# Spreading x by 128-partition transfers, and taking a block's rows and lookups later in the slot, in a recommender tower on one core

## The reference

```
e = stack([tbl_f[ids[:, f]] for f in range(32)], axis=1)      # (1024, 32, 16)
z_i[f, g] = x0[f] * h[g];  y = relu(W_i @ z_i + b_i)          # 128 outputs
layer 0: h = x (32 rows);  layer 1: h = upper half of y0 (64);  layer 2: h = upper half of y1 (64)
kept: lower halves of y0 and y1, all of y2; summed over the 16 columns e -> 256 values
h = concat([kept, dense_ctx (16)]); h = relu(h @ W_top1 + b); h = relu(h @ W_top2 + b); y = h @ W_top3
```

## Time and profile before

| | us |
|---|---|
| runs of the kernel before | 1099.53, 1104.21, 1105.62; median 1104.21 |
| the profiled execution | 1104.94, span 1103.1 |
| busy: PE | 1003.6 (91%) |
| busy: DVE | 840.5 (76%) |
| busy: POOL | 822.1 (75%) |
| busy: ACT | 470.1 (43%) |
| mean granted clock of PE, as a share of full speed | 0.969 |
| moved by DMA | 184.54 MB, mean 167 GB/s |

### The profile page before, as it was taken

The page is one execution under the profiler, slowest core; times in us unless marked ns, Lnnn a source line. Parts: engine busy times, 40 slices in busy tenths (PEclk is TensorE's granted clock), DMA queues, the critical chain, the costliest instruction groups (busy, mean ns, idle before and its releaser), DMA issues.

```text
span 1103.1 us, 11677 instructions
## 1 busy us (share of the span) xinstructions
PE 1003.6 (91%) x3089; PEld 572.8 (52%) x3089; DVE 840.5 (76%) x747; ACT 470.1 (43%) x587; POOL 822.1 (75%) x524
## 2 busy tenths in 40 slices
PE   3257889999997999998999989998899999999998
PEld 2223445555554555554555545554455555555565
DVE  5234768887785889888688869888478878888882
ACT  0123444444443444444345444444344444444453
POOL 6645778887877978887898878887788866656650
PEclk9579999999998999999999999999899999999999
DMA  6079989899896888899988899899688998999300
GB/s 119 10 159 208 200 174 205 188 194 193 168 195 139 184 180 186 183 196 190 184 172 185 186 182 184 182 191 196 143 179 179 195 202 188 192 198 196 86 1 0
DMA packets 111813, 184.54 MB, mean 167 GB/s; under 512 B 19571, under 2 KB 24179, under 8 KB 111541
## 3 DMA queue, kind: packets, MB, share of 16 engines
q1 hardware_dynamic: 103604, 182.24, 78.4%
q0 software_dynamic: 8192, 2.11, 2.0%
HBM read 181.15 MB, written 3.15 MB: 167 GB/s over the span
## 4 chain that ended last, share of the span: by engine, by line
POOL 38%; issue 28%; PE 23%; DVE 4%; SPq 2%; DMA 2%; ACT 1%; POOLq 0%; DVEq 0%
POOL low L490 22%; PE y L605 14%; POOL looked_up L480 13%; PE y L613 5%; PE y L628 3%; POOL tail_parts L498 2%; DMA spread<-xcols 1%; DVE unsplit L1046 1%; DVE prod L1046 1%; SPq L406 1%; SPq L424 1%; DVE low L1054 0%; PE xT L577 0%; PE y L709 0%; DMA xcols<-xrows 0%
## 5 line engine op out<-in xcount | busy, mean ns | idle before, releaser
L490 POOL TENSOR_TENSOR low<-unsplit,high 128x1024 fp32r<-128x1024 f32 x221 | 530.8, 2408 | 149.2 <-ACT high L809 145.8
L605 PE MATMUL y<-prod,w1T 128*128 128x512 f32 x1024 | 481.2, 598 | 5.0 <-ACT kept L801 2.7
L1046 DVE TENSOR_TENSOR prod<-spread,h 128x1024 f32<-128x1024 f32 x288 | 346.0, 1211 | 84.2 <-PE y L605 65.6
L809 ACT CAST high<-unsplit 128x1024 fp32r<-128x1024 f32 x224 | 233.9, 1046 | 293.4 <-DVE unsplit L1046 288.8
L1046 DVE TENSOR_TENSOR unsplit<-spread,h 128x1024 f32<-128x1024 f32 x224 | 271.3, 1211 | 100.1 <-ACT h L795 100.1
L480 POOL DMA_INDIRECT looked_up<-in_tbl,ids_now x256 | 249.1, 973 | 75.1 <-issue 66.8
L605 PEld LDWEIGHTS y<-prod,w1T 128*128 128x128 f32 x1024 | 193.3, 192 | 166.0 <-issue 145.3
L613 PE MATMUL y<-high,w2T_high 128*128 128x512 f32 x448 | 226.7, 506 | 6.6 <-ACT high L809 6.6
L628 PE MATMUL y<-low,w2T_high 128*128 128x512 f32 x448 | 207.0, 543 | 27.6 <-POOL low L490 27.3
L613 PE MATMUL y<-high,w2T_low 128*128 128x512 f32 x448 | 178.4, 398 | 0.0
L795 ACT ACTIVATE h<-y,bias 64x512 f32<-64x512 f32 x128 | 83.3, 651 | 165.4 <-PE y L605 161.4
(11 more groups left out here) (112 smaller groups left out, 418.6 us busy)
## 6 DMA issues: line engine op xcount, KB each, us to landing
spread<-xcols SPq DMA_DIRECT2D x256, 512.0 KB
shifted<-xcols SPq DMA_DIRECT2D x124, 256.0 KB
shifted_tail<-xcols SPq DMA_DIRECT2D x124, 64.0 KB
looked_up<-in_tbl,ids_now POOLq DMA_INDIRECT x256
xcols<-xrows SPq DMA_DIRECT2D x32, 96.0 KB
spread<-in_L_rec_W SPq DMA_DIRECT2D x3, 512.0 KB, 3.9
spread<-in_L_rec_W SPq DMA_DIRECT2D x1, 1024.0 KB
wt<-in_W_top SPq DMA_DIRECT2D x2, 512.0 KB, 10.1
```

Source lines behind the costliest of these rows:

```text
L490: pool.tensor_tensor(low[kind][r][:, :, :], unsplit[kind][r][:, :, :], high[kind][r][:, :, :].bitcast(F32), ALU.subtract).then_inc(s_low[k ...
L605: last = pe.matmul(y[:, :], w, z[:, c, :], start=(n == 0 and c == 0), stop=(item in (LAST0, LAST1) and c == ITEM - 1))
L809: act.copy(high[kind][r][:, :, :], unsplit[kind][r][:, :, :]).then_inc(s_high[kind], 1)
L1046: dve.tensor_tensor(z, x[:, ITEM * n:ITEM * (n + 1), :], b[:, :].unsqueeze(1).to_broadcast([P, ITEM, COLS]), ALU.mult).then_inc(s_made[kin ...
```

## The change

It has two parts, made together.

The first spreads x otherwise. In a group of four chunks each partition reads four rows of x that lie one behind the other in DRAM, 8 KB in one piece, by one DMA over all 128 partitions. Partition p of chunk c now has field c + 2 * (p // 8), modulo 32. Eight neighbouring partitions read the same bytes. The pairs of a field and a row of h are the same 2048 in another order, so the columns of W1 and W2 are put in that order before PE turns them: SP loads each with its first fields again behind the last (wrapped, 46 fields), and ACT makes eight copies of 128 x 512 into the prod buffers, from which PE turns. shifted likewise takes pieces of 8 KB, still by four DMAs of 32 partitions, and W0's arrangement and the first tile's factors (L1007) follow it.

The second moves work within the slot. ACT takes a block's rows and repeats the fields behind (2,2) instead of (2,0). In a block's first slot POOL begins the block behind (2,2) and TAIL, and makes two lookups behind each of (2,3), (2,4), (2,5) and (2,7). In the other three it makes two lookups ahead of all items, none behind (2,0) and (2,1), one behind (2,2), two behind (2,3), and one behind each of (2,4), (2,5), (2,7).

```diff
-LOOKUPS_AFTER = (0, 2, 2, 1, 1, 1, 1)
+LOOKUPS_AFTER = ((0, 0, 0, 2, 2, 2, 2), (0, 0, 1, 2, 1, 1, 1))
+LOOKUPS_FIRST = (0, 2)
...
-                for half in range(2):
-                    sp.dma_start(spread[k % 2][HALF * half:HALF * (half + 1), GROUP * g:GROUP * (g + 1), :],
-                                 bass.AP(x.tensor, x.offset + (2 * GROUP * g + half) * COLS,
-                                         [[0, HALF], [2 * COLS, GROUP], [1, COLS]])
-                                 ).then_inc(s_spread[k % 2][g], 16)
+                sp.dma_start(spread[k % 2][:, GROUP * g:GROUP * (g + 1), :],
+                             bass.AP(x.tensor, x.offset + GROUP * g * COLS,
+                                     [[2 * COLS, P // RUN], [0, RUN], [1, GROUP * COLS]])
+                             ).then_inc(s_spread[k % 2][g], 16)
...
                     sp.dma_start(shifted[FIELDS * j:FIELDS * (j + 1), :, :],
-                                 bass.AP(x.tensor, x.offset + j * COLS,
-                                         [[COLS, FIELDS], [GROUP * COLS, GROUP], [1, COLS]])
+                                 bass.AP(x.tensor, x.offset + GROUP * j * COLS,
+                                         [[COLS, FIELDS], [1, GROUP * COLS]])
...
+                if mine:
+                    look_up_some(LOOKUPS_FIRST[quarter > 0])
                 for n, item in enumerate(mine):
                     split_low(s, item)
                     if TAIL in items and item == (2, 2):
                         split_tail(s)
-                    if n == 1 and left and quarter == 0:
+                    if item == (2, 2) and left and quarter == 0:
                         begin(b)
-                    if n >= 1:
-                        for _ in range(LOOKUPS_AFTER[n]):
-                            if left:
-                                look_up(FIELDS // TILES_PER_BLOCK * quarter + left.pop(0))
+                    look_up_some(LOOKUPS_AFTER[quarter > 0][n])
...
+            for r, (raw, s_w, landed) in enumerate(((w1_raw, s_w1, 64), (w1_raw, s_w1, 64), (w2_raw, s_w2, 32), (w2_raw, s_w2, 32))):
+                act.wait_ge(s_w, landed)
+                for half in range(2):
+
+                    first = (2 * GROUP * (r % 2) + CHUNKS * half) * HALF
+                    last = act.copy(w_turned[r].rearrange("p (c h i j) -> p h c i j", h=2, i=HALF // RUN, j=RUN)[:, half],
+                                    bass.AP(raw.tensor, raw.offset + first,
+                                            [list(raw.ap[0]), [HALF, 2 * GROUP], [2 * HALF + RUN, HALF // RUN], [1, RUN]]))
+                last.then_inc(s_ordered, 1)
             act.wait_ge(s_biases, 5 * 16)
...
-                ready_after = (2, 0) if (2, 0) in items else (0, 0)
+                ready_after = (2, 2) if (2, 2) in items else (0, 0)
...
-                        dve.wait_ge(s_spread[t[1] % 2][n // (GROUP // ITEM)], 32 * uses_of_parity(t))
+                        dve.wait_ge(s_spread[t[1] % 2][n // (GROUP // ITEM)], 16 * uses_of_parity(t))
```

More of the change, by code:

```diff
@@ L53 @@
 COPY = 32
+RUN = 8
+WRAP = FIELDS - 2
 BYTES = 4
@@ L341, in dlrm_tower @@
         flat = lambda ap: ap.rearrange("p a b -> p (a b)")
[L342 to L345, removed]
+        w1_raw = flat(spread[0][:, 0:6, :])
+        w2_raw = flat(spread[0][:, 6:12, :])
+        w0_raw = flat(spread[0][:, 12:14, :])
+        w0_wide = flat(spread[1][:, 9:13, :])
         w0_dist = flat(spread[0][:, 14:16, :])
+        w_turned = [flat(prod[r][:, :, :]) for r in range(4)]
         dense_wide = flat(spread[1][:, 0:2, :]).rearrange("p (n c) -> p n c", c=P)
@@ L369, in _ @@
             sp.dma_start(w0_raw, w0[:, :]).then_inc(s_w0, 16)
-            sp.dma_start(w1_raw[0:HALF, :], w1[HALF:P, :]).then_inc(s_w1, 16)
-            sp.dma_start(w1_raw[HALF:P, :], w1[0:HALF, :]).then_inc(s_w1, 16)
-            sp.dma_start(w2_raw, w2[:, :]).then_inc(s_w2, 16)
+            ALL, MORE = FIELDS * HALF, (CHUNKS + WRAP - FIELDS) * HALF
+            for to, of in ((slice(0, ALL), slice(0, ALL)), (slice(ALL, ALL + MORE), slice(0, MORE))):
+                sp.dma_start(w1_raw[0:HALF, to], w1[HALF:P, of]).then_inc(s_w1, 16)
+                sp.dma_start(w1_raw[HALF:P, to], w1[0:HALF, of]).then_inc(s_w1, 16)
+            for to, of in ((slice(0, ALL), slice(0, ALL)), (slice(ALL, ALL + MORE), slice(0, MORE))):
+                sp.dma_start(w2_raw[:, to], w2[:, of]).then_inc(s_w2, 16)
             for to, of in ((bias0[HALF:P, :], b0[HALF:P]), (bias1[0:HALF, :], b1[HALF:P]),
@@ L508, in slot, with look_up_some @@
                 mine = of_kind(items, BY_POOL, plan.is_last(s))
+                def look_up_some(count):
+                    for _ in range(count):
+                        if left:
+                            look_up(FIELDS // TILES_PER_BLOCK * quarter + left.pop(0))
                 if TAIL in items and not mine:
                     split_tail(s)
+                if mine:
+                    look_up_some(LOOKUPS_FIRST[quarter > 0])
                 for n, item in enumerate(mine):
@@ L549, in _ @@
             pe.wait_ge(s_ident, 1)
-            pe.wait_ge(s_sym, 7)
+            pe.wait_ge(s_sym, 10)
             turn(0, GROUP, P, lambda c: w0_dist[:, P * c:P * (c + 1)])
             turn(1, 1, P, lambda c: w0_dist[:, P * GROUP:P * (GROUP + 1)])
-            pe.wait_ge(s_w1, 32)
-            for g in range(GROUPS):
-                turn(2 + g, GROUP, P, lambda c: w1_raw[:, P * (GROUP * g + c):P * (GROUP * g + c + 1)])
-            pe.wait_ge(s_w2, 16)
-            for g in range(GROUPS):
-                turn(2 + GROUPS + g, GROUP, P, lambda c: w2_raw[:, P * (GROUP * g + c):P * (GROUP * g + c + 1)])
+            for g in range(2 * GROUPS):
+                pe.wait_ge(s_ordered, g // 2 + 1)
+                turn(2 + g, GROUP, P, lambda c: w_turned[g // 2][:, P * (GROUP * (g % 2) + c):P * (GROUP * (g % 2) + c + 1)])
             pe.wait_ge(s_stored, PREP_GROUPS)
@@ L940, in _ @@
             H = FIELDS // 2
-            dve.tensor_copy(w0_dist[:, FIELDS:FIELDS * H].rearrange("p (d f) -> p d f", f=FIELDS),
-                            bass.AP(w0_wide.tensor, w0_wide.offset + 1,
-                                    [list(w0_wide.ap[0]), [1, H - 1], [2 * FIELDS + 1, FIELDS]])).then_inc(s_sym, 1)
+            for a in range(GROUP):
+                dve.tensor_copy(w0_dist[:, P * a:P * (a + 1)].rearrange("p (j f) -> p j f", f=FIELDS),
+                                bass.AP(w0_wide.tensor, w0_wide.offset + a,
+                                        [list(w0_wide.ap[0]), [GROUP, GROUP], [2 * FIELDS + 1, FIELDS]])).then_inc(s_sym, 1)
+            dve.wait_ge(s_sym, 3)
             dve.tensor_copy(w0_dist[:, 0:FIELDS], diagonal(w0_raw, FIELDS, 0, FIELDS)).then_inc(s_sym, 1)
@@ L1007, in _ @@
                 dve.tensor_copy(rotated[c].rearrange("p (e a f) -> p e a f", a=GROUP, f=FIELDS),
[L1008 to L1009 removed]
+                                bass.AP(unwrapped.tensor, unwrapped.offset + (c if c < GROUP else FIELDS // 2),
+                                        [list(unwrapped.ap[0]), [XROWS, QUAD], [GROUP if c < GROUP else 0, GROUP], [1, FIELDS]])
                                 ).then_inc(s_rotated, 1)
```

5 lines of the change are left out of this document (2 added, 3 removed).

## The result

The changed kernel takes 1094.53 us (median of 6 runs, 1093.26 to 1095.37), the kernel before 1103.08 beside it (6 runs): a ratio of 0.9921, with a 95% interval of 0.9896 to 0.9946. That is faster by 8.6 us, where I had forecast 29. It lies in the range of 1061 to 1096, but the likeliest case was wrong: less than a third of the gain came, and the time is that of rival (2). The profiled execution has a span of 1092.8, 10.3 less than before.

The account below looks back on a forecast made before the run. POOL was taken to lose time in waits, leaving 44.2 us above PE's floor of 29.31 per slot. Slots -20.5, filling -9, start 0: together -29.5 from 1104.9, predicting 1075 us, range 1061 to 1096.

Parts of the forecast that it names:

- the likeliest case: The forecast itself: 1075 us, its own range 1068 to 1085, chance 0.53.
- rival (2): Transfers stay at 213 GB/s, bound by rereading the same bytes; filling gains 0, stands stay 9.1: 1093 us; 0.14 with late ACT.
- The blocks: Slots of five blocks: 3.1 us per block above the floor instead of up to 5.8, 15.5 in all, between 9 and 22.
- held third slot: Block's third slot: DVE's addition held behind POOL's two low parts, POOL idles 5.1, low (2,2) late by 1.25 us.
- new stall in the second slot: Block's first two slots: low (2,7) 0.7 us late, then lookups ahead make low (2,0) 1.15 late.
- Rival (1): DVE's addition is let in behind one low part, so no third slot is held: 1067.5 us, chance 0.10.
- The transfers: Spread of x over 128 partitions moves at 370 GB/s instead of 213, bounds 213 and 385.
- The filling: While the pipeline fills, faster transfers shorten DVE's waits for shifted: 9 us less, bounds 0 and 14.2.
- The start: Extra weight loads and ACT's eight copies stay covered by the wait for first rows: 0; 14.5 us if ACT starts late.
- The stands: POOL's waits before lookups 114 and 227 shorten: slot 8 costs 3.0 instead of 9.4, slots 22 to 24 5.2 instead of 11.2.

Follow-up runs that it names:

- one_between: Changed kernel with one lookup of every plain slot moved from after GpSimd's fourth subtraction to between its first and second: 1081.97 us, ratio 0.9856 to before.
- o_plain: Kernel before with the change's block's first slot and ACT's copies behind (2,2), but old transfers and old lookups in the three plain slots: 1080.01 us, ratio 0.9786.
- src_rows: Changed kernel with the spread reading 128 different 8 KB rows of W1 in place of x: 1077.0 us (one run).
- src_reread: Changed kernel with the spread reading W1 in place of x, in the change's pattern of 8 partitions per stretch: 1090.1 us (one run).
- both_kept: o_plain with VectorE's addition of the kept part later (after (2,2)) and the change's transfers and reordered weights: 1063.83 us, ratio 0.9692 to before.
- plain_kept: o_plain with VectorE's addition of the kept part later (after (2,2) instead of (2,1)): 1068.08 us, ratio 0.9710 to before.
- one_more: Changed kernel with one lookup more at the start (field 0 of the first block again) and a wait for it: 1095.3 us.
- t_only: Kernel before with only the change's transfers and turned weights, order of rows and lookups as before: 1102.84 us, ratio 1.000.
- later_rows: Changed kernel with VectorE's addition of the kept part after (2,2) and the spread reading W1's distinct rows: 1085.5 us (one run).
- o_only: Kernel before with only the change's order of rows and lookups, transfers as before: 1094.34 us, ratio 0.9915.

## Why the prediction was right, and where it was wrong

*The blocks: right.* 15.5 forecast, 16.5 measured; in a late block 3.1 and 3.1. The held third slot came at 1.5 (forecast 1.25), with the addition at 5.2 and POOL's idle time at 5.11 (forecast 5.1). The new stall in the second slot came at 1.3, against 0.7 + 1.15; PE waits there for both low parts (0.32 at 414.44, 0.46 at 421.71). The closeness of the sum is partly luck: only three late blocks (slots 10 to 21) are whole and cost 3.1 each; the first block costs 5.8, 3.4 of it in its second slot, and slots 6, 7 and 9 cost 1.4. Rival (1), that one subtraction lets the addition in, is out by the 5.23 and by the 6.16 behind three; in the Trainium skill's words (SBUF — State Buffer, Who interferes with whom) the first to start holds the ports for its instruction, and no run here shows them passed on in between when the next subtraction is ready. one_between (2.44) and o_plain (1.90) show that it holds when the next isn't ready: the addition gets in behind one.

*The transfers: the step that failed.* "So partitions count, and the length of the piece doesn't", and from it "I take 370, as the nearest shape". W2 differed from W1's halves in partitions, as I said, but the spread differs from both in that eight partitions read the same bytes. I had named that as the bound at 213 and as rival (2), and gave it 0.14. src_rows and src_reread separate the two: with 128 partitions 1 MB lands in 6.1 us if the bytes are distinct and in 8.9 if they are reread, and the changed kernel's x moves at 207 GB/s, not 370. Partitions do count for distinct bytes (W1 came at 211 in halves, and at 410 GB/s and more in slices of src_rows, which reads it in 128 rows); that they decide alone was the error. (On the length of the piece the rows that bear are W1's halves and the old spread, 211 and 213, and not the first two.) The nearest shape has to be near in its source too. With distinct rows, the filling gained 8.3 of the 9 forecast.

*The filling: wrong by that step.* -9 forecast, -0.2 measured. The start, put at 0, cost 4.6 at the first transposes of the profiled run and nothing by the first of the 28 slots. A caution: the first transposes come either near 49 or near 54 us, whatever the kernel (before 49.29, after 53.92, but o_plain with the old transfers 54.12 and both_kept with the new ones 49.17). The late ones are those in which ACT's copies of the dense columns come near 50 (50.66 in the changed kernel, 50.86 in o_plain, 26.85 in plain_kept), but for one_more, whose first rows wait for the lookups; what holds the copies is open. The weights' reordering isn't the cause; t_only's 1.000 says that start and filling together brought nothing.

*The stands: wrong.* -12.4 forecast in two terms, -2.9 measured. The failed step is "if it waits for that lookup to land": with the engines 70% idle 5.9 us remain where that would leave 1.5. Whether faster transfers shorten a stand isn't shown: src_rows had 3.0 and 2.1 less in these slots than src_reread, but slot 8 read 38.49 in later_rows with the same distinct rows, and 36.15 in t_only with reread ones. The 2.7 that slots 22 to 25 did give come with the order (o_only, with the old transfers, gives 4.1 there, t_only 0.5), which moved the lookup behind (2,4).

*Not asked by me:* whether the plain slots' order was worth changing. I priced the block as one and never priced its halves; without the new lookups in the plain slots the order gives 24 us, and they cost 14.

## What to carry to other kernels

In these runs an operation of VectorE on SBUF alone waited through GpSimd's subtractions as long as they ran back to back: put something that isn't such an operation, a lookup's issue, between two of them where the other is due, and do that before moving the waiting one. When two edits come as one, price each place where an edit applies (here a block's first slot and its three others) by itself. Before pricing a transfer by a similar one, compare the source as well as the destination: here the same 1 MB took 6.1 us with distinct rows, 8.9 with each read eight times by neighbours. And look at the DMA share beside the rate: 112 GB/s at 0.52 was not slow memory but half of the engines at rest.

## What the runs showed of the hardware that was not expected

- Rereading doubles the time of a piece: 8 KB take 0.62 us when eight partitions read the same bytes (207 GB/s at a DMA share of 0.99), 0.31 when 128 read distinct ones, and still 0.61 when the readers are 8 or 16 partitions apart.
- The patterns that begin with a dimension of 8 kept 8 pieces in flight in place of 16: 112 GB/s at a share of 0.52, and 1.39 times the time before.
- A COPY with one input is held behind GpSimd's subtractions as an addition with two is (6.16 us behind three, for 0.4 to 0.6 unhindered), while products that read h from PSUM beside it keep their 1.21.
- POOL's two stands come before the same two lookups of the work in every version, with one lookup more too, and last 5.9 to 10.0 and 1.1 to 7.3 us; with the DMA engines 70% idle they are at their shortest, 5.9 and 1.1.
